# A fourth pair from parts in samples 4 to 6 of an adaptive-norm feed-forward kernel, with a reordered first stage

## The reference, cut to what matters

```python
# per sample b of 8: x[b] is 256 x 1024 (two tiles of 128 tokens)
h  = x[b] @ cond_w[id[b]].T                    # conditional product, fp32
h  = layernorm(h) * gamma + beta
q1 = fake_quant(h);  g = gelu(q1 @ fake_quant(w1).T + b1)
q3 = fake_quant(g);  x1 = x[b] + q3 @ fake_quant(w3).T + b3
y  = x1 @ base_w.T + bias + scale * (x1 @ A.T) @ B.T     # LoRA of sample b
# heads from rms-normed y: 16 residual logits, 4 pre, 4 post
# residual logits -> 50 Sinkhorn iterations; then mixing of four streams
```

## Time and profile before

| | |
|---|---|
| runs shown | 777.39, 776.84, 773.73 us |
| median | 776.84 us |
| profiled execution | 774.06 us |
| its span, first to last instruction | 772.3 us |
| mean granted TensorE clock | 0.971 of full |
| TensorE matmul busy | 711.6 us (92%) |
| VectorE busy | 555.5 us (72%) |
| ScalarE busy | 370.2 us (48%) |
| DMA | 125.40 MB, 162 GB/s over the span |

### The profile page before, as it was taken

One profiled execution on the slowest core, in us unless ns is written; L12 is line 12 of the kernel. 1 busy time (PEld: TensorE's weight loads), 2 busy tenths in 40 slices (PEclk: granted clock), 3 DMA queues, 4 the chain that ended last, 5 costly groups with the idle time before them and its releaser, 6 DMA issues.

```text
span 772.3 us, 10300 instructions
## 1 busy us (share of the span) xinstructions
PE 711.6 (92%) x3251; PEld 475.1 (62%) x3276; DVE 555.5 (72%) x1931; ACT 370.2 (48%) x646; POOL 68.2 (9%) x40
## 2 busy tenths in 40 slices
PE   8978799999999999989999899999999994999957
PEld 5443344274565656434665688887888883567656
DVE  4558776608888889697875504316899998999985
ACT  1242535314556473642643735435434442799614
POOL 0000200200201102452113000000000000000000
PEclk9989899999999999999999999999999998899989
DMA  7959995324544463556041133033032167756306
GB/s 298 409 173 325 259 379 191 123 82 143 210 162 169 163 219 137 181 214 227 5 164 55 61 104 124 1 123 119 5 124 81 44 204 242 233 194 206 122 1 217
DMA packets 54846, 125.40 MB, mean 162 GB/s; under 512 B 8324, under 2 KB 34052, under 8 KB 49289
## 3 DMA queue, kind: packets, MB, share of 16 engines
q1 hardware_dynamic: 53496, 122.02, 45.9%
q10 hardware_dynamic: 1296, 2.74, 0.9%
HBM read 99.01 MB, written 25.73 MB: 162 GB/s over the span
## 4 chain that ended last, share of the span: by engine, by line
PE 54%; DVE 30%; ACT 6%; DMA 5%; issue 3%; SPq 1%; ACTq 0%; DVEq 0%
PE PS L1159 18%; PE PS L984 10%; PE PS L1047 9%; DMA stage<-w_dram 4%; DVE kprod L1679 4%; PE PS L973 4%; DVE ksum L1683 4%; DVE hbuf L1384 2%; DVE ka L1686 2%; DVE kb L1686 2%; PE PS L1147 2%; PE PS L1311 2%; PE PS L1081 2%; DVE hbuf L1402 2%; DVE gbuf L1427 1%
## 5 line engine op out<-in xcount | busy, mean ns | idle before, releaser
L984 PE MATMUL PS<-w_raw,x_raw 128*128 128x512 f32 x336 | 156.2, 620 | 1.3 <-DMA w_raw<-cond_w_dram 0.8
L984 PEld LDWEIGHTS PS<-w_raw,x_raw 128*128 128x128 f32 x336 | 65.1, 199 | 76.7 <-issue 76.3
L1159 PE MATMUL PS<-w_hi,xT_hi 128*128 128x512 f32 x256 | 102.4, 400 | 0.0
L1159 PE MATMUL PS<-w_hi,xT_lo 128*128 128x512 f32 x256 | 100.1, 391 | 0.0
L1159 PE MATMUL PS<-w_lo,xT_hi 128*128 128x512 f32 x256 | 99.9, 390 | 0.0
L584 POOL TENSOR_TENSOR xres<-xres,vecs 128x1024 f32<-128x1024 f32 x16 | 43.0, 2707 | 313.5 <-DMA xres<-x_tok_dram 313.5
L1494 DVE TENSOR_TENSOR xT_lo<-PS,xT_hi 128x512 fp32r<-128x512 f32 x32 | 20.5, 682 | 66.6 <-ACT xT_hi L736 66.6
L1683 DVE TENSOR_REDUCE ksum<-kprod 128x16 f32<-128x64 f32 x392 | 66.3, 211 | 0.0
L1047 PE MATMUL PS<-w3q,qT 128*128 128x512 bf16 x243 | 56.6, 379 | 2.4 <-ACT qT L665 1.7
L1047 PE MATMUL PS<-w1q,qT 128*128 128x512 bf16 x244 | 56.5, 379 | 2.3 <-ACT qT L665 1.7
L1159 PEld LDWEIGHTS PS<-w_hi,xT_lo 128*128 128x128 f32 x256 | 48.0, 188 | 10.3
(11 more groups left out here) (202 smaller groups left out, 1362.9 us busy)
## 6 DMA issues: line engine op xcount, KB each, us to landing
w_raw<-cond_w_dram SPq DMA_DIRECT2D x31, 1024.0 KB, 5.6
x_raw<-x_tr_dram SPq DMA_DIRECT2D x32, 256.0 KB, 6.3
stage<-w_dram SPq DMA_DIRECT2D x16, 512.0 KB, 13.2
xres<-x_tok_dram SPq DMA_DIRECT2D x8, 1024.0 KB, 8.2
x_scratch<-x1buf SPq DMA_DIRECT2D x16, 512.0 KB, 6.4
x1n<-x_scratch SPq DMA_DIRECT2D x16, 512.0 KB, 6.3
y_scratch<-y SPq DMA_DIRECT2D x16, 512.0 KB, 3.1
stage<-base_w_nat_dram SPq DMA_DIRECT2D x8, 512.0 KB, 10.7
```

Of the source, the lines that this page charges most:

```text
L984: mm = pe.matmul(PS[:, 2 * t + h, :], x_raw[pr][:, c, t * P:(t + 1) * P], w_raw[pr][:, c, h * H2:(h + 1) * H2], start=(pr == 0 and c == 0) ...
L1159: pe.matmul(PS[:, 2 * t + h, :], xx[:, c, t * P:(t + 1) * P], ws[c // 2][:, c % 2, h * H2:(h + 1) * H2], start=(c == 0 and xx is xT_hi and ...
```

## The change

- `FIRST` becomes (3, 3, 3, 4): pair 2 goes by parts from sample 3, pair 3 from sample 4. On ScalarE the high parts of pair 3 stand before those of the next sample's first two pairs; on VectorE its low parts stand behind the second `finish_w3`. All high inputs live in `w_lo[3]`, pair 3's high weights in `w_hi[3]`.
- A pair 0 waits for each evacuated tile by itself (`bank_free`), not for both.
- The weight scales are spread on chip: GpSimd multiplies the identity by each column of scales (into `x1buf`), TensorE multiplies ones by that (`spread_scales`), and ScalarE evacuates (`evac_scales`). The DRAM scratch and its two DMAs each way are gone.
- The first stage is reordered on all engines: samples 0 and 1 go ahead of w3's stage tiles; the last stage tile and the second spread come in `step_a(2)`.
- The splits of the LoRA rows move into sample 2; `composites_1` moves to the end of sample 4, `composites_2` to sample 5, the heads' stores and loads to sample 6, and `store_head_rows` behind the load of sample 7's second pair. The wait for those stores is at `split_hi(2)`, not `split_hi(0)`.

```diff
-    FIRST = (3, 3, 4, NB)
+    FIRST = (3, 3, 3, 4)
+    HEADS_1, HEADS_2, HEADS_3 = 4, 5, 6
+        LATE_BANKS = (6, 7, 5, 4, 5, 4, 5, 5)
         def stage_bank(m):
-            return T_BANK + (m % 4 if m < KC + 4 else (m + 1) % 2)
+            return T_BANK + m % 4 if m < KC else LATE_BANKS[m - KC]
# SyncE
             load_w(1, 0)
+            load_w(1, 1)
             load_stage(KC)
             load_stage(KC + 1)
-            load_w(1, 1)
+            load_w(1, 2)
             load_stage(KC + 2)
             load_stage(KC + 3)
-            store_scales(0)
-            load_scales(0, V_SW1)
-            load_w(1, 2)
...
             def step_a_base(s):
...
                 load_w(s + 1, 1)
+                store_head_rows()
                 load_base(3)
# GpSimd
+            for w in range(2):
+                pool.wait_ge(st_inv, KC * (w + 1))
+                for c in range(KC):
+                    ins = nc.gpsimd.tensor_scalar(x1buf[w][:, c * P:(c + 1) * P], ident[:, :],
+                                                  wsc[:, 1, KC * w + c:KC * w + c + 1], None, ALU.mult)
+                ins.then_inc(diag_set, 1)
# ScalarE
             def split_hi(pr):
-                if pr == 0:
+                if pr == PAIRS - 2:
                     act.wait_ge(all_st, 64)
+            def evac_scales(w, v):
+                act.wait_ge(sc_mm, w + 1)
+                nc.scalar.activation(vecs[:, v, :].rearrange("p (b n) -> p b n", b=2), PS[:, O_BANK:O_BANK + 2, :],
+                                     ACT.Copy).then_inc(sc_ev, 1)
             evac_l0(0, 1)
+            ln_root(0, 0)
+            quant1(0, 0)
+            evac_scales(0, V_SW1)
+            evac_T(0, 0, 1)
             evac_stage(KC)
             evac_stage(KC + 1)
-            ln_root(0, 0)
...
             def step_a(s):
+                quant1(s - 1, 0)
                 if s == 2:
-                    ln_root(s - 1, 0)
-                quant1(s - 1, 0)
+                    rows_high()
                 pair_high(s, 2)
...
                 evac_T(s - 1, 0, 1)
+                if s < GUEST:
+                    pair_high(s, 3)
                 pair_high(s + 1, 0)
                 pair_high(s + 1, 1)
# TensorE
+                def bank_free(c, t, h):
+                    if pr == 0 and c == 0 and h == 0:
+                        wait(pe, l0_evac, NTOK * (s - 1) + t + 1)
+            def spread_scales(w):
+                pe.wait_ge(id_zero, 2)
+                pe.wait_ge(diag_set, w + 1)
+                pe.wait_ge(st_ev if w == 0 else o1_done, KC if w == 0 else 4)
+                for h in range(2):
+                    mm = pe.matmul(PS[:, O_BANK + h, :], ones[:, :], x1buf[w][:, h * H2:(h + 1) * H2], start=True, stop=True)
+                mm.then_inc(sc_mm, 1)
+            l0(1, 0)
+            spread_scales(0)
+            l0(1, 1)
+            transposes(0, 0, 1)
             stage_T(KC)
             stage_T(KC + 1)
-            l0(1, 0)
+            l0(1, 2)
             stage_T(KC + 2)
...
             def step_a(s):
                 transposes(s - 2, 0, 3)
+                if s == 2:
+                    stage_T(KC + 7)
+                    spread_scales(1)
                 l0(s, 0)
-                if s == 3:
+                if s == HEADS_2:
                     composites_2()
...
-                if s == 2:
+                if s == HEADS_1:
                     composites_1()
# VectorE
-            quantise_stage(KC)
-            quantise_stage(KC + 2)
             dve.wait_ge(vec_ld, 16 * 2)
             layer_norm(0, 0)
+            quantise_stage(KC)
+            layer_norm(0, 1)
+            quantise_stage(KC + 2)
             quantise_stage(KC + 4)
-            layer_norm(0, 1)
+            dve.wait_ge(sc_ev, 1)
+            scale_w1(0, 0)
             quantise_stage(KC + 6)
...
             def step_a(s):
...
                 finish_w3(s - 2, 1)
+                if s < GUEST:
+                    pair_low(s, 3)
                 pair_low(s + 1, 0)
                 pair_low(s + 1, 1)
                 finish_w1(s - 1, 0)
```

More of the change, by code:

```diff
@@ L71, in adaln_ffn @@
         ST = len(stage)
-        bnat, vsb = stage[ST - 2], stage[ST - 1]
+        vsb, bnat = stage[0], stage[1]
         part_s.close()
@@ L82, in adaln_ffn @@
         part_n = ctx.enter_context(ExitStack())
+        for i in range(2 * PAIRS - 4):
+            sb_in(part_n, f"below_heads{i}", [P, D], F32)
         heads_in = sb_in(part_n, "heads_in", [NB * RANK, NH], F32)
@@ L230, in adaln_ffn @@
         vec_ld, bias_ld, ids_ld, ones_set = sem("vec_ld"), sem("bias_ld"), sem("ids_ld"), sem("ones_set")
-        high = [sem(f"high{i}") for i in range(PAIRS - 1)]
-        low = [sem(f"low{i}") for i in range(PAIRS - 1)]
+        high = [sem(f"high{i}") for i in range(PAIRS)]
+        low = [sem(f"low{i}") for i in range(PAIRS)]
         id_zero, id_set, id16_set = sem("id_zero"), sem("id_set"), sem("id16_set")
@@ L326, in load_nat @@
                 sp.dma_start(stage[c][:, :], base_w_nat[c]).then_inc(st_ld[c], 16)
-            def store_scales(w):
-                sp.wait_ge(st_inv, KC * (w + 1))
-                with nc.allow_non_contiguous_dma(reason="1024 scales, once"):
-                    sp.dma_start(sw_dram[w].rearrange("c p -> p c"), wsc[:, 1, KC * w:KC * (w + 1)]).then_inc(swst, 16)
-            def load_scales(w, v):
-                sp.wait_ge(swst, 16 * (w + 1))
-                sp.dma_start(vecs[:, v, :], sw_dram[w:w + 1].rearrange("w c p -> w (c p)").to_broadcast([P, D])
-                             ).then_inc(swld, 16)
             def load_rows():
@@ L386, in _ @@
             load_w(1, 0)
+            load_w(1, 1)
             load_stage(KC)
             load_stage(KC + 1)
-            load_w(1, 1)
+            load_w(1, 2)
             load_stage(KC + 2)
             load_stage(KC + 3)
-            store_scales(0)
-            load_scales(0, V_SW1)
-            load_w(1, 2)
-            load_stage(KC + 4)
-            load_stage(KC + 5)
-            load_w(1, 3)
-            load_stage(KC + 6)
-            load_stage(KC + 7)
+            load_w(1, 3)
+            for m in range(KC + 4, 2 * KC):
+                load_stage(m)
+            load_w(2, 0)
+            load_w(2, 1)
+            load_xres(0)
+            load_w(2, 2)
             sp.wait_ge(st_T, KC + 4)
@@ L402, in _ @@
             load_rows()
-            load_xres(0)
-            load_w(2, 0)
-            load_nat(0)
-            load_nat(1)
-            load_w(2, 1)
-            store_scales(1)
-            load_nat(2)
-            load_nat(3)
-            load_w(2, 2)
-            load_scales(1, V_SW3)
-            load_nat(4)
-            load_nat(5)
             load_w(2, 3)
-            load_nat(6)
-            load_nat(7)
             def step_a(s):
+                nat = KC - 2 if s == HEADS_1 else 0
                 load_w(s + 1, 0)
+                for c in range(0, nat, 2):
+                    load_nat(c)
                 load_w(s + 1, 1)
                 store_x1(s - 2, 0)
+                for c in range(1, nat, 2):
+                    load_nat(c)
                 load_w(s + 1, 2)
@@ L425, in step_a @@
                 load_w(s + 1, 3)
+                for c in range(nat, KC if nat else 0):
+                    load_nat(c)
                 load_xres(s - 1)
@@ L707, in _, with rows_high @@
             act.dma_start(bcol[:, :], bias_col).then_inc(misc_ld, 16)
-            act.dma_start(bnat[:, :], lora_b_nat).then_inc(misc_ld, 16)
+            def rows_high():
+                act.wait_ge(all_ld, 16 * (2 * NB + 1))
+                nc.scalar.activation(all_hi[:, :], all_in[:, :], ACT.Copy, scale=all_scale[:, 0:1]).then_inc(all_high, 1)
+                nc.scalar.activation(one_hi[:, :], one_in[:, :], ACT.Copy).then_inc(all_high, 1)
             def pair_high(s, pr):
@@ L1043, in product @@
                 pe.wait_ge(ev, NTOK * s + t + 1)
+                if s == 0 and which == 3:
+                    pe.wait_ge(st_ev, 2 * KC)
+                    pe.wait_ge(sc_ev, 2)
                 for h in range(2):
@@ L1086, in composites_2 @@
                 pe.wait_ge(v_sb, 1)
+                pe.wait_ge(misc_ld, 5 * 16)
                 for c in range(KC):
@@ L1108, in step_a @@
                 transposes(s - 2, 1, 3)
-                if s != 3:
+                if s != HEADS_2:
                     l0(s, 1)
```

128 lines of the change are left out of this document (62 added, 66 removed).

## The result

The changed kernel takes 784.20 us (median of 4 runs, 781.34 to 785.04). The kernel before, on the same chip, takes 776.97 (773.73 to 777.39). The ratio is 1.0099, 95% interval 1.0074 to 1.0125: slower by 7.2 us. The profiled execution of the changed kernel took 781.34 us with a span of 779.4; against 774.06 and 772.3 before, that is 7.1 us more of span. So the two traces can be held against each other; both are executions near the lower end of their kernel's runs, 2.9 us under its median.

The account below looks back on a forecast made before the run. VectorE's chain with round trips (39.5 us) was taken as nearly as long as TensorE's 41.2 us step. Terms -10.1 + 4.0 - 0.9 + 4.4 + 2.8 + 2.0 + 1.2 + 2.2 = +5.6 gave 779.7 to 782.4; forecast 780, range 767 to 787.

Parts of the forecast that it names:

- First stage: Up to sample 2's first second-layer product: reordering and scales spread on chip bring it to some 96 from 106.15, -10.1 us.
- the clock: Behind the first stage's two new gaps: TensorE's clock falls after each, +4.0 us for two, between 0 and 5.7.
- Samples 2 and 3: Sample 2 loses a 0.89 us wait as the long head products leave, -0.9; sample 3 becomes 41.1 us against 45.1.
- Sample 4: No slack in VectorE's chain: the fourth pair's parts add +2.8 us, a clock fall before the long head products +2.0.
- Sample 5: Short head products and two more pairs from parts make VectorE's quantisation 4.3 us late: 49.3 us against 40.9.
- Sample 6: The fourth pair's low parts come some 1.3 us late, which the cheaper pair gives back: 0.
- Sample 7: GpSimd's base weights collide with VectorE's addition, +1.2 us; the head rows' stores delay ScalarE's third base split, +2.2.
- a collision: Sample 7: VectorE's second bias addition meets GpSimd's low parts on the shared ports, +1.2 us (0 to 2.4).
- the upper bound that I had given: Sample 7: the head rows' stores land 5.1 us after issue and move the next quantisation by +3.6 us.
- Rival 3: Sample 7: stores at the upper bound, GpSimd's last split then collides with VectorE's last norms; 783 to 787 us, chance 0.17.
- Rival 2: Samples 3 to 6: VectorE isn't the limit, all four pairs bring their 1.3 us; some 762 to 765 us, chance 0.18.
- Rival 1: Whole chain as laid out, but clock up in all three gaps and stores landed at once; 772.4 to 775.1 us, chance 0.20.

Follow-up runs that it names:

- the fastest kernel: Changed kernel with only its new first stage kept, pairs from parts, head products and head rows' stores as before (the table's last column): 766.98 us, 0.9893 of the kernel before.
- three runs: The fastest kernel with the fourth pair from parts (773.83 us) or the third in sample 3 too (770.23); the changed kernel with its fourth pair whole (773.90).
- four parts: The fastest kernel with the fourth pair of samples 4 to 6 also from parts: 773.83 us, 0.9967 of the kernel before.
- the scales by the scratch: Changed kernel with its new order kept, but the scales of both quantised layers through the scratch in DRAM again: 785.98 us, 1.0122 of the kernel before.

## Why the prediction was right, and where its steps failed

The forecast was 780 us, range 767 to 787, from +5.6 on the profiled time; measured +7.3 on the profiled time, +7.2 on the medians. The sign and the cause were right: VectorE's chain and the head rows' stores take back more than the first stage gives. That the size is so near is partly luck: the first stage came out 2.4 us better than forecast, samples 5 to 7 together 4.6 us worse. By its own steps:

- **First stage:** forecast -10.1 and +4.0 of clock, measured -8.5. The layout stood: gaps of 2.77 and 2.69 us against 2.7 and 3.1, TensorE at 97.7 with one price for clock (1.8 us on the pair behind the first gap) against 96 without any. (The terms written out behind 68.8 add up to 95.5, which would have made it -10.6.) The term that was mis-sized is the clock: after the second gap it stayed at 1.00. The gaps were also not "as long as" the 4.19 and 3.33 us that the term leaned on; the 2.15 us of the earlier trace rows, behind which the next pair took 8.78 us, alone spoke for it.
- **Samples 2 and 3:** forecast -0.9 without the moved 13.8 us, and -4.0 for sample 3; measured -14.9 with them, and -3.8. Right.
- **Sample 4:** forecast +2.8, +2.0 of clock and the 13.8 moved in, +18.6; measured +18.1. TensorE's wait ahead of the long products is 2.31 us against 0.89 and they take 15.59 us against 13.9. Right.
- **Sample 5:** forecast +8.4, measured +10.2. The chain was right: from the second tile's transposes to the end the sample takes 31.40 us where sample 3 of the kernel before took 26.99, 4.4 more against the 4.3 of the sum. What had no term is a fall of the clock ahead of it, behind the short head products: from the first transposes to the second 19.66 us against 18.09, 1.6 of the 1.8 us (last section). The product behind the wait of 2.81 us took 4.70 us at the lower clock and not 3.6, but VectorE came to its result at 278.31 without a wait, so that cost nothing at the end. The lines after (first fence) and before (second):

```profile
233.98 0.62 PE L1000 MATMUL PS<-ident,gbuf 128*128 128x128 f16 x8
...
253.64 0.61 PE L1000 MATMUL PS<-ident,gbuf 128*128 128x128 f16 x8
```

```profile
156.73 0.62 PE L993 MATMUL PS<-ident,gbuf 128*128 128x128 f16 x8
...
174.82 0.61 PE L993 MATMUL PS<-ident,gbuf 128*128 128x128 f16 x8
```

- **Sample 6:** forecast 0, measured +0.8, and here the step was wrong in kind. I said that the cheaper pair gives back what VectorE's lateness costs. It doesn't: the same edit costs 1.1 us in the fastest kernel too, at full clock. And its end was late: ScalarE's base split then stood ahead of the evacuation for sample 7 (a wait of 2.17 us where there was 0.28).
- **Sample 7:** forecast +1.2 for a collision and +2.2 for the stores, measured +5.4. The collision missed the addition, which took 1.23 us, and met a later step of the norm, which took 3.10 us where others like it take 1.28:

```profile
331.02 3.10 DVE L1409 SCALAR_TENSOR_TENSOR hbuf<-hbuf,lnst,vecs 128x1024 f32<-128x1024 f32 x1
```

  VectorE then waited 9.31 us behind the stores, so it cost nothing. The stores cost more than the upper bound that I had given: TensorE's wait is 4.2 us longer, against 3.6. They landed 5.6 us after their issue, near my 5.1, but I had counted their issue from the old time of GpSimd's second split, and that split itself started 1.8 us after the sample's first transposes and not 1.0 ahead of them. So 2.8 us of VectorE's lateness in sample 6 went through ScalarE, GpSimd and SyncE into this wait.
- **Rival 3** named the stores at their upper end, 783 to 787, and the time lies there; its other half isn't there: GpSimd's last base split meets VectorE's norm in both kernels (an instruction of 1.28 us takes 4.23 us after, 5.61 before), and adds nothing. **Rival 2** (VectorE isn't the limit) is excluded by three runs: +6.8, +3.3 and -10.3 us where it wanted -3.9, -1.3 and +3.9. **Rival 1** wanted the clock kept in all gaps and the stores landed at once; of that only the clock behind the second gap of the first stage came true.

## What to carry to other kernels

A cheaper form on the busiest engine pays only while the engine that prepares it has time left. Here TensorE was busy for 39.8 of 41.2 us, VectorE with its round trips for 39.5: three pairs from parts fit, and the fourth cost 2.9 and 3.6 us in samples 4 and 5 to save 1.1 and 0.9. A lateness that starts on such an engine is passed on through queues to places that the edit never touched, so a moved store must be priced from the new times of all that its queue waits for, and from the bytes that lie ahead of it.

## What the runs showed of the hardware that I had not expected

- **A tiny store behind large loads.** A store of 24 numbers took 9.7 us to release its waiter with a load of 1 MB more ahead of it, 6.6 us with that load behind it; both times the release came within 0.3 us of the landing of the last load ahead.
- **The clock falls without a wait, in most traces, and the sample pays.** Behind the short head products, with TensorE never idle, the pair from parts ran at the lower clock for some 3 us in 11 of the 14 traces, those of the changed kernel and of the fastest one among them, and not in those of the kernel before, of four parts and of the scales by the scratch, where the sequence of work is the same. A stretch of the changed kernel, and matmuls of one shape in the kernel before and in the fastest:

```profile
244.00:247.00 3.00, 3.00 (x9) 2.29 (x9) 0.00 (x0) 0.00 (x0) 0.00 (x0) 0.55 0.39 147
```

```profile
166.03 0.40 PE L973 MATMUL PS<-w_low,w_lo 128*128 128x512 f32 x1
```

```profile
158.13 0.63 PE L980 MATMUL PS<-w_lo,x_low 128*128 128x512 f32 x1
```

  Its price is seen where nothing else differs up to there: sample 3 takes 46.62 us with the fall (the fastest kernel, first fence: the first transposes, VectorE's first use of the product behind the pair, the next sample's transposes) and 45.07 without (four parts, second fence). VectorE waits for TensorE 1.55 us longer, and the whole chain behind it shifts:

```profile
148.15 0.62 PE L1001 MATMUL PS<-ident,gbuf 128*128 128x128 f16 x8
...
166.32 0.75 DVE L1476 SCALAR_TENSOR_TENSOR x1buf<-PS,q2st,vecs 128x512 f32<-128x512 f32 x1 [8.39 <-PE PS L1069]
...
194.77 0.61 PE L1001 MATMUL PS<-ident,gbuf 128*128 128x128 f16 x8
```

```profile
148.24 0.62 PE L1001 MATMUL PS<-ident,gbuf 128*128 128x128 f16 x8
...
164.87 0.75 DVE L1476 SCALAR_TENSOR_TENSOR x1buf<-PS,q2st,vecs 128x512 f32<-128x512 f32 x1 [6.84 <-PE PS L1069]
...
193.31 0.61 PE L1001 MATMUL PS<-ident,gbuf 128*128 128x128 f16 x8
```

  So 1.6 of the 7.1 us between the traces after and before, and the 1.5 us by which the table's last column has sample 3 above the first, are this fall. What decides it stays open; it wasn't tried.
- **A wait as long as another may keep the clock.** 2.77 us at 41.9 was followed by the lower level, 2.69 us at 70.2 was not; and of two waits in the same place of the same work, 2.40 us was followed by it and 2.38 us was not.
